# Attention and FFN block on one core: the next batch's x and context turned by VectorE and a pass through memory instead of by TensorE

## What is computed

```python
def _L0_xattn_ref(q, k, v, Wq, Wk, Wv, bv, Wo, bo):
    qh = (q @ Wq.T).reshape(Bq, Sq, N_HEADS, hd).transpose(0, 2, 1, 3)
    kh = (k @ Wk.T).reshape(Bq, Sq, N_HEADS, hd).transpose(0, 2, 1, 3)
    vh = (v @ Wv.T + bv).reshape(Bq, Sq, N_HEADS, hd).transpose(0, 2, 1, 3)
    scores = jnp.einsum('bhsd,bhtd->bhst', qh, kh) * scale
    mask = jnp.triu(jnp.ones((Sq, Sq), dtype=bool), k=0).at[0, 0].set(False)
    probs = jax.nn.softmax(jnp.where(mask, -jnp.inf, scores), axis=-1)
    out = jnp.einsum('bhst,bhtd->bhsd', probs, vh)
    return out.transpose(0, 2, 1, 3).reshape(Bq, Sq, HIDDEN_F) @ Wo.T + bo
x = x + _L0_xattn_ref(_layernorm(x), ctx_1024, ctx_1024, ...)
x = x + _L0_ffn_ref(_layernorm(x), ...)
```

## Time and profile before

| | us |
|---|---|
| median of 3 runs | 2705.21 (2700.21 to 2708.8) |
| profiled execution | 2700.74 |
| its span | 2699.0 |
| TensorE busy in the span | 2581.1 (96%) |
| VectorE busy | 1737.9 (64%) |
| ScalarE busy | 1029.4 (38%) |
| POOL busy | 787.4 (29%) |

### The profile page before, as it was taken

One profiled execution on the slowest core, in us unless ns is written; L12 is line 12 of the kernel. 1 busy time (PEld: TensorE's weight loads), 2 busy tenths in 40 slices (PEclk: granted clock), 3 DMA queues, 4 the chain that ended last, 5 costly groups with the idle time before them and its releaser, 6 DMA issues. The chain is left out here.

```text
span 2699.0 us, 44806 instructions
## 1 busy us (share of the span) xinstructions
PE 2581.1 (96%) x14018; PEld 1916.2 (71%) x14018; DVE 1737.9 (64%) x3406; ACT 1029.4 (38%) x1903; POOL 787.4 (29%) x1495
## 2 busy tenths in 40 slices
...
DMA packets 133699, 232.36 MB, mean 86 GB/s; under 512 B 20499, under 2 KB 22547, under 8 KB 133156
## 3 DMA queue, kind: packets, MB, share of 16 engines
...
...
## 5 line engine op out<-in xcount | busy, mean ns | idle before, releaser
L742 ACT ACTIVATE probs<-bank 128x512 f32<-128x512 f32 x640 | 359.0, 596 | 306.9 <-PE bank L534 299.9
L1143 PE MATMUL h_bank<-x2T_hi,fcT 128*128 128x512 f32 x1024 | 406.4, 397 | 0.9 <-ACT scale_row L1219 0.9
L1144 PE MATMUL h_bank<-x2T_lo,fcT 128*128 128x512 f32 x1024 | 406.9, 397 | 0.0
L1155 PE MATMUL y_bank<-projT,a_hi 128*128 128x512 f32 x1024 | 404.3, 395 | 0.0
L1157 PE MATMUL y_bank<-projT,a_lo 128*128 128x512 f32 x1024 | 403.9, 394 | 0.0
L1227 ACT ACTIVATE relu<-h_bank,scale_fc 128x512 f32<-128x512 f32 x256 | 176.1, 688 | 517.4 <-PE h_bank L1147 517.4
L435 POOL TENSOR_SCALAR_AFFINE_SELECT probs<-probs 128x256 f32<-128x256 f32 (+1 forms) x640 | 228.1, 367 | 242.9 <-ACT probs L742 236.6
L509 PE MATMUL bank<-stack 96*128 96x512 f32 (+3 forms) x1024 | 266.9, 338 | 18.5 <-DMA stack<-stage 14.7
L534 PE MATMUL bank<-stack 98*128 98x512 f32 (+3 forms) x1024 | 265.6, 343 | 15.8 <-DMA stack<-m_stage 15.1
L804 DVE TENSOR_REDUCE maxima<-bank 128x1 f32<-128x512 f32 x256 | 175.7, 686 | 138.2 <-PE bank L513 134.8
L1342 DVE CAST a_hi<-act_sq 128x512 fp32r<-128x512 f32 x256 | 108.4, 423 | 240.6 <-ACT act_sq L1232 240.6
...
## 6 DMA issues: line engine op xcount, KB each, us to landing
stack<-stage SPq DMA_DIRECT2D x768, 128.0 KB, 2.3
xc_rows<-in_x_dram SPq DMA_DIRECT2D x16, 1024.0 KB, 5.3
x_res<-in_x_dram SPq DMA_DIRECT2D x16, 1024.0 KB, 5.4
...
x_in_sb<-x SPq DMA_DIRECT2D x16, 1024.0 KB, 5.7
x_res<-x SPq DMA_DIRECT2D x16, 1024.0 KB, 7.8
...
xc_rows<-in_ctx_dram SPq DMA_DIRECT2D x15, 1024.0 KB, 5.3
```

The source lines that it names most:

```text
L742: act.activation(probs[:, s[2], :], t_bank[u % 2][:, :], ACT.Exp, scale=SCALE).then_inc(exp_done, 1)
L1143: pe.matmul(h_bank[b % 2][:, :], fcT[:, k, cols], xT_hi[:, k, :], start=k == 0, stop=False)
L1144: pe.matmul(h_bank[b % 2][:, :], fcT[:, k, cols], xT_lo[:, k, :], start=False, stop=False)
L1155: pe.matmul(y_bank[j][:, :], a_hi[:, b % RING, P * j:P * j + P], projT[:, b, :], start=b == 0, stop=False)
```

## The change

The transposes XT and CT leave TensorE in all steady batches (the first batch's, in the setup, stay). In their place VectorE turns 32 by 32 blocks of the normalised x (XTURN 0 to 3) and of the context (CTURN 0 to 3) into `x_res`; SyncE stores the 1 MB of `x_res` to memory (X_STORE, C_STORE) and loads it back with four DMAs of 32 partitions each, so that the blocks land turned in `xc_rows` (X_BACK, C_BACK). ScalarE copies the high part from there (XH, CH) and VectorE subtracts for the low part.

For this X_LOAD and C_LOAD move to the start of the batch, the context into `acc`, whose next use on POOL waits for CTURN. The LayerNorm's statistics move ahead of group 1 and its application into group 1. XRES comes only after X_STORE, and its bias add on POOL (XBIAS) after the last T. PART Q 0 moves up behind T(2,0) and T(2,1), Q 0 ahead of S(3,9). `attn` shares its first two tiles with `cT_hi` and `cT_lo`, so CH 0 and 1 wait for `oa_done`.

```diff
-        ("XRES",), ("V", 0), ("S", 0, 0), ("PART", "Q", 1, 0), ("S", 0, 1), ("S", 0, 2), ("PART", "Q", 1, 1),
...
+        ("S", 0, 6), ("K", 1), ("S", 0, 7), ("S", 0, 8), ("PART", "V", 1, 0), ("S", 0, 9),
+        ("PART", "V", 1, 1), ("V", 1), ("STACK", 1, 0), ("M", 0), ("CTURN", 0), ("CTURN", 1),
+        ("SEND", 0), ("V", 2), ("CTURN", 2), ("CTURN", 3), ("LN_STATS", 0), ("LN_STATS", 1), ("PART", "Q", 2, 0), ("STACK", 1, 1), ("PART", "Q", 2, 1), ("T", 0, 0), ("T", 0, 1),
+        ("C_STORE",), ("LN_STATS", 2), ("S", 1, 0), ("S", 1, 1), ("LN_STATS", 3), ("Q", 2), ("T", 0, 2), ("S", 1, 2), ("LN_VAR",), ("LN_RSTD",),
+        ("S", 1, 3), ("T", 0, 3), ("PART", "K", 2, 0), ("S", 1, 4), ("T", 0, 4), ("LN_NEWTON",), ("T", 0, 5),
...
+        ("S", 1, 8), ("S", 1, 9), ("PART", "V", 3, 1), ("T", 0, 9), ("V", 3), ("M", 1), ("LN_APPLY", 3), ("XTURN", 0),
+        ("XTURN", 1), ("XTURN", 2), ("XTURN", 3), ("X_STORE",), ("PART", "Q", 3, 0), ("SEND", 1), ("PV", 0, 0), ("PV", 0, 1), ("PV", 0, 3), ("PV", 0, 2), ("STACK", 2, 1),
...
+        ("PART", "K", 3, 1), ("S", 2, 8), ("K", 3), ("S", 2, 9), ("T", 1, 9), ("STACK", 3, 0), ("M", 2),
+        ("XH", 0), ("NT", 0), ("NR", 0), ("XH", 1), ("NB", 0), ("PV", 1, 0), ("PV", 1, 1), ("NM", 0, 0), ("XH", 2), ("XH", 3), ("STACK", 3, 1),
+        ("SEND", 2), ("XRES",), ("C_BACK",), ("PV", 1, 3), ("PV", 1, 2),
+        ("T", 2, 0), ("PART", "Q", 0, 0), ("S", 3, 0), ("NH", 0, 0), ("T", 2, 1), ("PART", "Q", 0, 1), ("T", 2, 2), ("NC", 1), ("ONES", 1), ("NL", 0, 0),
...
+        def moved_tile(k):
+
+            return xc_rows[:, :, :].rearrange("p g (j k t) -> p k j g t", j=TT, k=KT)[:, k]
...
+            def load_back(turned, moved):
+
+                for q in range(4):
+                    sp.dma_start(xc_rows[32 * q:32 * q + 32, :, :],
+                                 turned[:, q, :].rearrange("(g c) e -> c g e", c=32)).then_inc(moved, 16)
...
+                    elif s[0] == "C_LOAD":
+                        wait_alone(sp, sp_passed, (ones_done, START + i * (GROUPS - 1)))
+                        load_rows(acc, ctx_in, i + 1, c_loaded)
                     elif s[0] == "X_LOAD":
+                        wait_alone(sp, sp_passed, (mm_full, first), (c_ready, START + i * KT))
+                        load_rows(xc_rows, x, i + 1, x_loaded)
...
+                    elif s[0] == "X_STORE":
+                        wait_alone(sp, sp_passed, (x_turned, i * TT + TT))
+                        sp.dma_start(x_turned_dram, x_res[:, :, :]).then_inc(x_stored, 16)
+                    elif s[0] == "X_BACK":
+                        wait_alone(sp, sp_passed, (x_stored, i * 16 + 16))
+                        load_back(x_turned_dram, x_moved)
...
+                    elif s[0] == "XH":
+                        if s[1] == 0:
+                            act.wait_ge(x_moved, i * BACK + BACK)
+                        act.activation(by_32(xT_hi[:, s[1], :]), moved_tile(s[1]), ACT.Copy
+                                       ).then_inc(x_hi, 1)
...
+                        dve.transpose(x_res[:, :, :].rearrange("p q (j k t) -> p j k q t", j=TT, k=KT)[:, s[1]],
+                                      (xc_rows if s[0] == "XTURN" else acc)[:, s[1], :]
+                                      .rearrange("p (k q t) -> p k q t", k=KT, q=4)
...
+                    elif s[0] == "XH":
+                        dve.wait_ge(x_hi, i * KT + s[1] + 1)
+                        dve.tensor_tensor(by_32(xT_lo[:, s[1], :]), moved_tile(s[1]),
+                                          by_32(xT_hi[:, s[1], :]).bitcast(F32), ALU.subtract).then_inc(x_ready, 1)
```

More of the change, by code:

```diff
@@ L58, in batch_steps @@
     steps = [
[3 rows of a table removed]
-        ("STACK", 1, 0), ("M", 0), ("V", 2), ("SEND", 0), ("PART", "Q", 2, 0), ("STACK", 1, 1), ("PART", "Q", 2, 1),
[17 rows of a table removed]
[3 rows of a table added]
+        ("PART", "V", 1, 1), ("V", 1), ("STACK", 1, 0), ("M", 0), ("CTURN", 0), ("CTURN", 1),
+        ("SEND", 0), ("V", 2), ("CTURN", 2), ("CTURN", 3), ("LN_STATS", 0), ("LN_STATS", 1), ("PART", "Q", 2, 0), ("STACK", 1, 1), ("PART", "Q", 2, 1), ("T", 0, 0), ("T", 0, 1),
[5 rows of a table added]
+        ("XTURN", 1), ("XTURN", 2), ("XTURN", 3), ("X_STORE",), ("PART", "Q", 3, 0), ("SEND", 1), ("PV", 0, 0), ("PV", 0, 1), ("PV", 0, 3), ("PV", 0, 2), ("STACK", 2, 1),
[5 rows of a table added]
+        ("SEND", 2), ("XRES",), ("C_BACK",), ("PV", 1, 3), ("PV", 1, 2),
[4 rows of a table added]
         ("PV", 2, 2), ("OA", 0, 0), ("NM", 1, 0), ("NH", 1, 0), ("T", 3, 0), ("T", 3, 1), ("NL", 1, 0), ("OA", 1, 0),
         ("T", 3, 2), ("T", 3, 3), ("ONES", 2), ("NT", 2), ("T", 3, 4), ("T", 3, 5), ("NR", 2), ("OA", 1, 1),
[1 row of a table removed]
[1 row of a table added]
         ("OA", 3, 0), ("OA", 2, 0), ("OA", 3, 1), ("NB", 2), ("PV", 3, 0), ("NM", 2, 0), ("PV", 3, 1), ("NH", 2, 0),
[1 row of a table removed]
[1 row of a table added]
         ("NB", 3), ("NM", 3, 0), ("NH", 3, 0), ("NM", 3, 1), ("OC", 0), ("NL", 3, 0), ("K", 0), ("NH", 3, 1),
[3 rows of a table removed]
-    ]
-    return steps if more else [s for s in steps if not is_next(s, True) and s[0] not in ("X_LOAD", "C_LOAD")]
[2 rows of a table added]
+    ]
+    moves = ("X_LOAD", "C_LOAD", "X_STORE", "C_STORE", "X_BACK", "C_BACK")
+    return steps if more else [s for s in steps if not is_next(s, True) and s[0] not in moves]
 def low_parts_later(steps):
@@ L114, in is_next @@
 def is_next(step, in_batch):
-    return in_batch and (step[0] in ("LN_STATS", "LN_VAR", "LN_RSTD", "LN_NEWTON", "LN_APPLY", "XT", "CT")
+    return in_batch and (step[0] in ("LN_STATS", "LN_VAR", "LN_RSTD", "LN_NEWTON", "LN_APPLY", "XTURN", "CTURN", "XH",
+                                    "CH")
                          or step[:2] in (("Q", 0), ("K", 0), ("STACK", 0)) or step[:3] == ("PART", "Q", 0))
```

82 lines of the change are left out of this document (60 added, 22 removed), and 38 rows, old and new, of the table steps.

## The result

The changed kernel takes 2838.78 us (median of 4 runs, 2836.28 to 2841.97) beside 2703.4 us of the kernel before (4 runs): a ratio of 1.0502, 95% interval 1.0486 to 1.0518. It is 135 us slower, where 104 were forecast. The profiled execution spans 2836.2 us; its mean granted clock is 0.961.

What follows compares the result with a forecast made beforehand. TensorE was taken to set the pace. Terms 2.4 + 1.5 + 0.8 - 0.3 + 2.5 = 6.9 us a batch, times 15 = 104, on the median of 2705.21 gave 2809 us, range 2690 to 2880.

Steps and rivals of the forecast that it cites:

- The direction and its reason: TensorE's removed transposes: most lie in waits, only CT 0 and 1 don't; worth about 1.0 us a batch, not 4.8.
- The clock: TensorE behind M(2) and two new waits: granted clock falls, costing 2.5 us a batch, from about 1 to 7.
- X_STORE ahead of STACK(2,1): SyncE's queue after M(1): stacks wait behind the store, S(2,5) waits for them; 1.5 us a batch, from 0.2 to 3.0.
- VectorE from M(0) to M(1): Added CTURN and LayerNorm work delays S(1,0) and T(0,5); TensorE 2.4 us late a batch, bounds 1.4 and 4.
- M(2) to S(3,0): XH copies delay SEND 2, late low parts delay Q 0 and S(3,0); +0.8 us a batch, from -0.3 to +1.8.
- The end: End of the batch: CT 0 and 1 go, -1.0; XBIAS and CH up to +0.9; taken as -0.3 us.
- The rival in which the clock stays up: Whole loop: the waits come without a clock fall, 4.4 us a batch, 2771 us; chance 0.24.
- The wash: VectorE's new work fits its idle time, only one stall shows; 0 to 0.5 us a batch, 2705 to 2712; chance 0.06.
- Filling the gap: No late stack, T(0,5) doesn't wait, Q 0 fills the gap behind T(2,0); -20 us, 2686; chance 0.13.
- the return of TensorE's whole busy time: All eight transpose groups come back one for one, 72 us, giving 2633; chance 0.05.

Runs made afterwards that it cites:

- e8: Kernel before, with CT 0 and CT 1 alone turning one block in place of four, 6 transposes fewer a batch: 2687.99 us, ratio 0.9944.
- e10: Kernel before, with XT 0 to 3 turning one block in place of four, 12 transposes fewer a batch: 2757.68 us, ratio 1.0208.
- e1: Changed kernel with X_STORE issued behind STACK(2,1) on SyncE instead of ahead of it: 2779.16 us, ratio 1.0283.
- e4: Changed kernel, but the loop loads only the first 128 of 512 rows of the next context: 2817.68 us, ratio 1.0426.
- e3: Changed kernel plus twelve useless transposes on TensorE behind M(2), where XT 1 to 3 stood: 2807.53 us, ratio 1.0386.
- e11: As e6, with C_LOAD issued ahead of X_LOAD: 2728.19 us, ratio 1.0089.
- e6: Changed kernel with X_STORE behind STACK(2,1), Q 0's two PARTs put back to their old places, and twelve useless transposes behind M(2): 2722.03 us, ratio 1.0071.

## Why the prediction was right, point by point

**The direction and its reason: right.** TensorE's busy time was not worth its length. The step from the last batch's rows (only CT 0 and 1 stand in no wait) is shown by e8 and e10: one cut gains 0.6 us a batch, the other leaves S(3,0) where it was.

**The clock: right in kind, too small.** I took 2.5 us a batch from bounds of 1 to 7; it is about 3.6 in the changed kernel, 2.5 of it behind M(2) (22.45 us in the mean for 19.99), and 4.1 in e10, where nothing else changed. What I had not seen is that the late stack at S(2,5) lowers the clock too: this is why e1 gave 4.0 us where the wait was 2.16. I listed the clock as one term behind M(2). In ten of 14 batches it came behind that stall too. The last batch was a poor source for the size: that batch took 95.74 us at 0.91 before, and takes 91.19 at 1.00 in the changed kernel, though T(2,0) and S(3,0) wait 0.97 and 1.91 us in it:

```profile
1670.00:1674.00 4.00, 1.69 (x10) 0.97 (x14) 0.57 (x1) 1.40 (x3) 2.51 (x6) 1.00 0.90 205
1674.00:1678.00 4.00, 3.90 (x25) 2.16 (x24) 3.04 (x8) 2.72 (x6) 1.90 (x5) 1.00 0.87 199
```

What decides whether the clock falls behind such a gap or holds is open.

**X_STORE ahead of STACK(2,1): right, at 2.16 for 1.5.** X_STORE went out 4.3 us behind M(1) (4.4 to 4.9 forecast; 4.4 + 3.8 + 2.3 makes 10.5 and not 10.4 for the last stack, which moves nothing), and the six stacks took 4.93 to issue (before 3.81):

```profile
296.96 0.35 SPq L418 DMA_DIRECT2D x_turned<-x_res  x1
297.51 4.93 SPq L370 DMA_DIRECT2D stack<-stage  x6
```

**VectorE from M(0) to M(1): right in size, 2.6 in the mean (1.8 to 3.9) for 2.4, but by luck: two causes share it, and I had one.** VectorE's part is 1.75 (e4, and the shortest batches of e3 and e11: 19.10 to 19.12 for 17.35). It is 0.9 us late at S(1,0)'s reduction (e4) where I had 1.4; a CTURN takes 0.64 us (1.28 for two), and the earlier trace rows, from which I took 0.73, are of a tile of 32 partitions, not of this size. T(0,5) is late behind LN_RSTD as forecast, but waits 0.6 to 0.8 us and not about 2. The rest, 0.8 in the mean, is T(0,0), which I had missed: SEND 0's small rows land 4.4 us after their issue with the DMA engines full of x, context and stacks (DMA share 1.08 from 272 to 279 us). Two loads had made me think only of CTURN 0 being late, which it is, 1.55 us a batch; taking that wait away gained nothing (e11):

```profile
stack<-m_stage ACTq DMA_DIRECT2D x2, 8.0 KB, 4.4
```

The Trainium skill (DMA: Bandwidth & Descriptors, "Issuing engines are not separate DMA queues") says that DMAs of all issuing engines run on the same 16 engines and interleave; this case agrees, since these two were issued by ScalarE, and T(0,0) waits for them no longer once SyncE's load of the context is small (e4).

**M(2) to S(3,0): one half wrong, the other too small.** SEND 2 was not late. I had put it behind four XH copies, 2.9 us after M(2), and it went out at 1.05 us, ahead of copies that stand before it in the program:

```profile
313.38 0.61 ACT L774 ACTIVATE xT_hi<-xc_rows 128x512 fp32r<-128x512 f32 x1
313.89 0.51 ACTq L754 DMA_DIRECT2D stack<-m_stage  x1
313.90 1.13 ACT L774 ACTIVATE xT_hi<-xc_rows 128x512 fp32r<-128x512 f32 x2
314.43 0.72 ACTq L754 DMA_DIRECT2D stack<-m_stage  x1
314.94 0.61 ACT L774 ACTIVATE xT_hi<-xc_rows 128x512 fp32r<-128x512 f32 x1
```

So T(2,0) came at 4.17 us, not at 6.2, and the gap behind it was the longer; it waited 1.02 us, as forecast, but because XT 1 and 2 no longer stood ahead of it (e10, with them quartered: 1.00). The low parts were late as I had feared: the four took 1.12, 0.63 and 2.07 for two and were done at 7.4 us, for 6.1 unhindered and 7.5 to 8.5 hindered. Q 0 started then, and S(3,0) at 9.3, near the bound of 9.4. The rule in the Trainium skill (SBUF — State Buffer, "Who interferes with whom") would have each of them held up beside a POOL instruction that reads SBUF; the rows agree for POOL's adds, while the one of 0.63, at 315.97, lay within POOL's copies (315.95 to 316.97). The net cost was 2.17 us at full clock (19.99 - 17.82, e3) where I took 0.8 and gave 1.8 as the bound. I had credited Q 0's matmuls done early with 0.93; e6, which has them later, takes 18.82, so the early Q 0 lost 1.2 there and 0.5 at the end (26.13 for 25.65), and earned nothing. Part of the rest is M(3), which waits 0.79 for the maxima since Q 0 stands ahead of S(3,9), and which I had costed at nothing.

**The end: right.** -0.8 us for -0.3, inside -1.0 to +0.9.

**The sum.** The waits come to 6.1 us at full clock (2.6 + 2.1 + 2.2 - 0.8) for 4.4, the clock to 3.6 for 2.5; 9.7 for 6.9, against the batch of 94.80. So the store, M(2) and the clock were each put too small, the end's cost too large, and the range of 2690 to 2880 had room for it. I had counted 15 batches. The 14 periods of the steady loop are 9.5 us longer each (104.5 - 95.0), 133 us; the first batch's end comes 7.3 us later, and the last batch went 4.6 us the other way. Of the 135 us, e1 took back 60, Q 0's place 20 and the useless transposes 37. What remains in e6 is 1.5 us in the batch of the table (96.30 - 94.80; 1.9 in the mean): 2.05 at M(0) to M(1) and 1.00 behind M(2), less 0.27 ahead of it and 1.28 at the end.

The rival in which the clock stays up (2771) had the same waits, 4.4 for 6.1, and is out by the clock, 0.95 to 0.97 in all 14 batches. The wash (up to 2712) is out by 127 us. Filling the gap (2686) is out by the waits at T(0,5) and S(2,5), which it excluded, and the return of TensorE's whole busy time (2633) by e10.
